# A vision layer on one core: the value weighing and the side work of an attention loop regrouped into four-step packets, and the loop over images written out

## The chip, the core and the metric

The kernel runs on one core of a Trainium2 chip. The metric is the device time of one execution in microseconds (us), lower being better. TensorE is called PE here, VectorE DVE, ScalarE ACT, GpSimd POOL, and SyncE, which issues most DMAs, SP.

## What is computed

Eight images of 3x512x512 are cut into 1024 patches each, embedded to 256 channels, sent through attention with 8 heads, and then through a layer whose second matrix is chosen per token among eight experts:

```python
h = embedded + pos                                   # 8 x 1024 x 256
x = _layernorm(h)                                    # attention's own norm follows
normed = (x - mu) / jnp.sqrt(var + EPS) * ln_gamma + ln_beta
q, k, v = jnp.split(normed @ W_qkv.T, 3, axis=-1)
gate = sigmoid(x @ W_gate.T + b_gate)
scores = jnp.einsum('bhid,bhjd->bhij', q, k) * D ** (-0.5)
attn = softmax(scores, axis=-1)
out = jnp.einsum('bhij,bhid->bhjd', attn, v) * gate  # note: weighs by the row's index i
h = h + x + out @ W_final.T + b_final
H = gelu(layernorm(h) @ W1 + b1)                     # 1024 wide
probs = softmax(H @ Wg + bg);  e = argmax(probs)
h = h + probs[e] * (H @ Wd[e] + bd[e])
```

## The kernel before

Everything is float32; scores, hidden products and the expert products go through PE in its one-pass form (`F32R`), the others as two half products, so that the profile counts two matmuls for each such call. Each engine has its own instruction stream, written by hand in the order in which it runs, and the streams meet by semaphores alone. PE, DVE and ACT take their instructions strictly in that order, so an instruction that waits holds everything behind it.

**The attention loop.** An image `b` has 64 steps `k`: two groups of four heads, eight blocks `i` of 128 rows in each group, four heads `hh`. A step is one chain over three engines. `score(b, k)` on PE makes a 128x1024 block of scores in two banks of PSUM (L477). DVE takes its row maximum (`reduce_max`, L1029). ACT makes the exponentials with their sums (L842). There are two pairs of banks (`SR = 2`), so `score(k)` waits for the exponentials of step `k - 2`. The exponentials stay in SBUF in `pr`, eight blocks deep.

**The weighing.** After four steps (one row block `i`, four heads) DVE divides the values by the sums, `scale_v` (a reciprocal, L945, and a multiply, L948, which raises `vs_ready`). It stands behind the maximum of step `4i + 4` (`SCALE_AT`). PE's `weigh(b, i, j)` for the quarters `j` = 0 to 3 adds `vs.T @ pr` to the output (L491). Each call is four products of 32 columns that run side by side in the array; the text calls one call a block. Quarter 0 waits for `vs_ready`.

**Side work.** The other products that an image needs are laid between the steps by tables. In the first half (k = 0 to 31) stand the projections of the second head group (`QK1_AT`, `project`, L465, in two halves `c`, at k = 0 to 7), and the embedding of the next image (`EMBED_AT`, `embed`, L444, 24 parts at k = 8 to 31). In the second half (k = 32 to 63) stand the gates (`GATE_AT`, L511), the transposes of the next image (`TURN_AT`, `turn`, L456) and its projections for the first head group (`QK0_AT`, L465). They share two spare PSUM banks: part `j` of a kind waits until part `j - 2` has been read. ACT reads a transposed part (`turned`, L772 and L775) and a projection (`high`, L785), in its stream behind the exponentials of the step of the part. DVE makes the rest of a projection (`low`, L936), two steps later (`LOW1_AT`, `LOW0_AT`), and reads a finished embedding (`embedded`, L917).

**Around the steps.** Between k = 31 and 32 stands the router part of the image before (L540 to L576). Between k = 63 and the next image's k = 0 stand `values`, the last weighing (i = 15), the final projection and the first gates. After the last image come the sorting of tokens and 72 slots of expert products, which this change leaves alone.

**The loop over images.** `over_images` writes images 0 and 7 out, and runs a hardware loop of three rounds over two images each between them (1 and 2, 3 and 4, 5 and 6):

```python
body(0, 0, False, True)
with eng.Fori(0, (IMAGES - 2) // 2) as j:
    body(j * 2 + 1, 1, True, True)
    body(j * 2 + 2, 0, True, True)
body(IMAGES - 1, (IMAGES - 1) % 2, True, False)
```

Of the kernel before, what the change touches and what calls it, by code (L numbers as in the profile page):

```python
# [27 lines left out]
IMAGES = 8  # L28
TOKENS = 1024
TILES = TOKENS // P  # L30
# [7 lines left out]
STEPS = HEADS * TILES  # L38
# [9 lines left out]
G_STEPS = STEPS // GROUPS  # L48
# [7 lines left out]
def vit_layer_kernel(nc, x, w_patch, pos_in, pos_w1, pos_w2, pos_bias, ln_gamma, ln_beta, w_qk, w_v,  # L56
# [7 lines left out]
    with ExitStack() as ctx:  # L64
# [149 lines left out]
        def over_images(eng, body):  # L214


            body(0, 0, False, True)
            with eng.Fori(0, (IMAGES - 2) // 2) as j:
                body(j * 2 + 1, 1, True, True)
                body(j * 2 + 2, 0, True, True)  # L220
            body(IMAGES - 1, (IMAGES - 1) % 2, True, False)

        def over_pairs(eng, count, body):

            body(0)
            with eng.Fori(1, count) as j:
# [6 lines left out]
        QK1_AT = {m: divmod(m, 2) for m in range(8)}  # L233
        EMBED_AT = {8 + m: divmod(m, 3) for m in range(24)}
        GATE_AT = {G_STEPS + 3 + m: divmod(m, 2) for m in range(4)}
        TURN_AT = {G_STEPS + 7 + j: j for j in range(8)}
        QK0_AT = {G_STEPS + 17 + 3 * j + c: (j, c) for j in range(4) for c in range(2)}

        LOW1_AT = {k + 2: j for k, (j, c) in QK1_AT.items() if c == 1}
        LOW0_AT = {k + 2: j for k, (j, c) in QK0_AT.items() if c == 1}  # L240
        NORM_AT = {2 + t: t for t in range(TILES)}
        SCALE_AT = {4 * i + 4: i for i in range(15) if i != 7}
        WEIGH_AT = {k: [(i, j) for i in range(15) if i != 7 for j in range(4)
                        if k == min(4 * i + 5 + j // 2 * 2, (i // TILES + 1) * G_STEPS - 1)] for k in range(STEPS)}
# [171 lines left out]
        def _(pe):  # L416
# [202 lines left out]
            def image(b, par, before, after):  # L619
# [15 lines left out]
                for k in range(STEPS):  # L635
# [14 lines left out]
                    score(b, k)  # L650
                    if before and k == G_STEPS + 1:
                        partial_logits(b - 1, 1, 0)
                    if before and k == G_STEPS + 2:
                        turn_logits(b - 1, 1, 1)
                    if k in QK1_AT:
                        j, c = QK1_AT[k]
# [3 lines left out]
                    if after and k in EMBED_AT:  # L660
                        t, part = EMBED_AT[k]
# [3 lines left out]
                    if k in GATE_AT:  # L665
                        hf, c = GATE_AT[k]
# [3 lines left out]
                    if after and k in TURN_AT:  # L670
                        if TURN_AT[k] < 2:
                            wait(pe, "g_tanh", b * 4 + 3 + TURN_AT[k])
                        turn(b + 1, TURN_AT[k])
                    if after and k in QK0_AT:
                        j, c = QK0_AT[k]
# [3 lines left out]
                    for gi, j in WEIGH_AT[k]:  # L679
                        weigh(b, gi, j)  # L680
# [542 lines left out]
```

How the kernel before makes its waits and increments, by code:

```python
        def wait(eng, name, value):  # L201
            if not isinstance(value, int) or value > 0:
                eng.wait_ge(S[name] if isinstance(name, str) else name, value)
# [1 line left out]
        def hold(eng, name, value):  # L206
            if not isinstance(value, int):
                value = eng.to_reg(value)
                eng.wait_ge(S["setup"], 1)
            wait(eng, name, value)
# [36 lines left out]
        @block.sync  # L249
# [50 lines left out]
                    load_rest(b + 1)  # L300
                load_stack(b, 1, before)
                if before:
                    for u in range(4, 16):
                        store_hidden(b - 1, u)
            over_images(sp, image)
            for u in range(16):
                store_hidden(IMAGES - 1, u)
            sp.wait_ge(S["lg_done"], 2 * IMAGES)
            sp.wait_ge(S["h_out"], 16 * IMAGES)
            for i in range(STAGED):
                sp.wait_ge(row_out[i], 16 * IMAGES * 16 // STAGED)
            sp.dma_start(bd_raw[:], b_down).then_inc(S["bd_raw_in"], 16)
            def load_down(j):
                for i in range(WD_BUFFERS):
                    hold(sp, "wd_low", j * WD_BUFFERS + i + 1 - WD_BUFFERS)
                    sp.dma_start(wd_raw[:, i], w_down[j * WD_BUFFERS + i]).then_inc(wd_in[i], 16)
            over_pairs(sp, WD_PIECES // WD_BUFFERS, load_down)
            sp.wait_ge(S["bd_low"], 1)
            sp.wait_ge(S["bd_zero"], 1)
            for part in range(2):
                for e in range(EXPERTS):
```

## Time and profile before

| | |
|---|---|
| median of 3 runs | 1952.97 us (1948.21 to 1954.45) |
| the profiled execution | 1954.93 us, span of the core 1952.8 us |
| PE busy | 1728.6 us, 89% of the span |
| DVE busy | 1151.3 us, 59% |
| ACT busy | 1012.5 us, 52% |
| mean granted TensorE clock | 0.954 of full speed |

The profile gives busy time by engine and line, the stretches between chosen points of the span with the granted clock, and the instructions in order of time. Averages over the span mix stages with different limits; the steps of the attention loop have to be read one stage at a time, by the starts of their scores.

### The profile page before, as it was taken

How to read it: one execution, taken by the hardware profiler on the slowest of the kernel's cores; microseconds unless marked ns; L12 is line 12 of the kernel's file. 1: busy time of each engine (PE TensorE's matmuls, PEld its weight loads, DVE VectorE, ACT ScalarE, POOL GpSimd, SP SyncE). 2: the span in 40 equal slices, each digit the busy share in tenths (PEclk: the TensorE clock that was granted, in tenths of full speed). 3: DMA queues.
4: the chain of work that ended last, by engine and by line, in shares of the span. 5: the costliest groups of instructions: out<-in, count | busy, mean ns of one | idle time of the engine just before them, and what ended most of it. 6: DMA issues, size and time to landing. Idle time of an engine off the chain costs nothing.

```text
span 1952.8 us, 32763 instructions
## 1 busy us (share of the span) xinstructions
PE 1728.6 (89%) x11396; PEld 1180.4 (60%) x11396; DVE 1151.3 (59%) x1899; ACT 1012.5 (52%) x1692; POOL 309.7 (16%) x239
## 2 busy tenths in 40 slices
PE   8587899999998999999899999999797724899998
PEld 4354456646655574566467555745363614899998
DVE  0347767467655856675667468566726278344443
ACT  1144756675574657566746656585666350222222
POOL 0200100200010020002000200200000061455554
PEclk9898999999999999999999999999899867899999
DMA  3133042313413140424033222413040160566663
GB/s 112 34 98 98 1 103 77 125 30 99 112 65 82 63 133 28 103 69 133 18 103 92 93 65 73 129 39 87 17 135 1 60 220 1 200 205 199 208 204 132
DMA packets 68112, 187.59 MB, mean 96 GB/s; under 512 B 14173, under 2 KB 14829, under 8 KB 67824
## 3 DMA queue, kind: packets, MB, share of 16 engines
q1 hardware_dynamic: 51952, 121.48, 22.0%
q0 software_dynamic: 16000, 63.98, 10.0%
q8 instruction: 101, 1.65, 0.4%
q14 instruction: 59, 0.48, 0.1%
HBM read 84.72 MB, written 51.38 MB: 70 GB/s over the span
## 4 chain that ended last, share of the span: by engine, by line
PE 72%; DVE 14%; issue 8%; ACT 4%; DMA 1%; SPq 1%; POOL 0%; DVEq 0%; ACTq 0%; POOLq 0%
PE ps L477 12%; PE ps L738 11%; PE ps L491 10%; PE ps L444 8%; DVE nmax L1029 6%; PE ps L548 3%; PE ps L465 3%; PE ps L726 3%; PE ps L549 3%; PE ps L550 3%; PE ps L527 3%; PE ps L505 3%; PE ps L576 3%; ACT pr L842 2%; DVE oh L1084 2%
## 5 line engine op out<-in xcount | busy, mean ns | idle before, releaser
L1029 DVE TENSOR_REDUCE nmax<-ps 128x1 f32<-128x1024 f32 x512 | 625.2, 1222 | 315.1 <-PE ps L477 305.5
L842 ACT ACTIVATE pr<-ps,nmax 128x1024 f32<-128x1024 f32 x512 | 569.9, 1113 | 295.8 <-DVE nmax L1029 290.6
L477 PE MATMUL ps<-stk,stq 96*128 96x512 f32 x1024 | 407.3, 480 | 80.2 <-ACT pr L842 54.1
L477 PEld LDWEIGHTS ps<-stk,stq 96*128 96x128 f32 x1024 | 168.5, 193 | 282.7 <-ACT pr L842 169.0
L491 PE MATMUL ps<-pr,vs 128*32 128x256 f32 x4096 | 275.9, 391 | 16.7 <-DVE vs L948 16.6
L738 PE MATMUL ps<-wd,hg 128*128 x1728 | 225.5, 287 | 0.0
L339 POOL TENSOR_SCALAR vare<-mv 128x8 f32<-128x8 f32 x24 | 5.7, 238 | 1349.8 <-DVE mv L903 1349.8
L738 PEld LDWEIGHTS ps<-wd,hg 128*128 128x128 f32 x1728 | 212.7, 192 | 0.0
L491 PEld LDWEIGHTS ps<-pr,vs 128*32 128x32 f32 x4096 | 109.8, 110 | 166.6 <-issue 75.5
L879 ACT ACTIVATE hg<-ps 128x512 fp32r<-128x512 f32 x144 | 78.5, 596 | 249.6 <-PE ps L726 249.6
L444 PE MATMUL ps<-wp,xt 128*128 128x256 f32 x768 | 198.3, 385 | 1.6 <-DMA xt<-x_in 0.8
L444 PEld LDWEIGHTS ps<-wp,xt 128*128 128x128 f32 x768 | 146.2, 192 | 32.6 <-DMA xt<-x_in 3.1
L811 ACT ACTIVATE ht<-ps,bf 128x512 f32<-128x512 f32 x128 | 88.3, 690 | 115.5 <-PE ps L550 115.5
L465 PE MATMUL ps<-nt,wqk 128*128 128x512 f32 x256 | 132.3, 602 | 3.9 <-DVE qk L936 3.2
L1148 DVE TENSOR_TENSOR hg<-ps,hg 128x512 fp32r<-128x512 f32 x144 | 93.0, 686 | 48.9 <-ACT hg L879 48.8
L548 PE MATMUL ps<-nt_high,wf 128*128 128x512 f32 x256 | 110.7, 432 | 1.7 <-DVE nt_low L985 1.4
L549 PE MATMUL ps<-nt_low,wf 128*128 128x512 f32 x256 | 101.9, 398 | 0.0
L550 PE MATMUL ps<-nt_high,wf 128*128 128x512 f32 x256 | 101.3, 396 | 0.0
L1155 DVE SCALAR_TENSOR_TENSOR rows<-ps,slot_prob,rows 128x256 f32<-128x256 f32 x72 | 34.8, 484 | 111.1 <-PE ps L740 111.1
L842 ACT ACTIVATION_READ_ACCUMULATOR pr<-ps,nmax 128x1 f32 x512 | 99.5, 194 | 0.0
L404 POOL DMA_INDIRECT out<-rows,slot_to x72 | 72.3, 1004 | 123.2 <-DVE rows L1155 116.3
L726 PE MATMUL ps<-ident,rows 128*128 128x128 f32 x576 | 76.4, 277 | 6.6 <-DMA rows<-token_rows,slot_from 6.6
(123 smaller groups left out, 1944.2 us busy)
## 6 DMA issues: line engine op xcount, KB each, us to landing
token_rows<-staged SPq DMA_DIRECT2D x128, 256.0 KB, 2.0
xt<-x_in SPq DMA_DIRECT2D x64, 384.0 KB, 3.1
stq<-qk SPq DMA_DIRECT2D x192, 128.0 KB, 2.4
stk<-qk SPq DMA_DIRECT2D x192, 128.0 KB, 2.5
token_rows<-hres POOLq DMA_DIRECT2D x8, 1024.0 KB, 5.2
wd_raw<-w_down SPq DMA_DIRECT2D x16, 512.0 KB, 4.0
rows<-token_rows,slot_from POOLq DMA_INDIRECT x72, 4.7
out<-rows,slot_to POOLq DMA_INDIRECT x72, 2.6
```

The source lines that it names most:

```text
L444: last = mm(spare(t)[:, 0:D], xt[:, t % 2, k, :], wp[:, k, :], start=(k == 0), stop=(k == KC - 1))
L465: last = mm(spare(j), wqk[:, c, w * D + g * P:w * D + (g + 1) * P], nt[:, c, hf * HALF:(hf + 1) * HALF], start=(c == 0), stop=(c == DC - 1))
L477: last = mm(ps[:, 2 * (k % SR) + j, :], stq[:, hh, i * P:(i + 1) * P], stk[:, hh, j * 512:(j + 1) * 512], start=True, stop=True)
L491: last = mm(ps[32 * hh:32 * hh + 32, O_BANK + j // 2, (j % 2) * D:(j % 2 + 1) * D], vs[:, gi % 2, hh, :], pr[:, (4 * gi + hh) % PR, j * D: ...
L548: mm(spare(bank), w_high, nt_high[:, c, half], start=(c == 0), stop=False)
L549: mm(spare(bank), w_high, nt_low[:, c, half], start=False, stop=False)
L550: last = mm(spare(bank), w_low, nt_high[:, c, half], start=False, stop=(c == DC - 1))
L726: last = nc.tensor.transpose(ps[:, 2 * (s % 2) + c, q * P:(q + 1) * P], rows[:, s % RING, (4 * c + q) * P:(4 * c + q + 1) * P], ident[:])
L738: mm(o, hg[:, s % 2, h_part, k, :], wd[:, w_part, bass.ds(e, 1), k, :], start=(k == 0 and h_part == w_part), stop=False)
L842: actv(pr[:, k % PR, :], ps[:, 2 * (k % SR):2 * (k % SR) + 2, :].rearrange("p a n -> p (a n)"), ACT.Exp, bias=nmax[:, k % 16:k % 16 + 1], ...
L1029: V.reduce_max(nmax[:, k % 16:k % 16 + 1], ps[:, 2 * (k % SR):2 * (k % SR) + 2, :].rearrange("p a n -> p (a n)"), AX_X, negate=True).then_ ...
L1148: V.tensor_tensor(hg[:, s % 2, 1, 4 * c:4 * c + 4, :].rearrange("p k n -> p (k n)"), ps[:, 2 * (s % 2) + c, :], high_part.bitcast(F32), AL ...
```

## The change

Three things change. Nothing is computed differently, and no instruction that does arithmetic is added or removed.

1. `WEIGH_AT`: the four blocks of a row block's weighing all stand in step `4i + 5`, and right behind its score, ahead of any side work. Before, two stood at the end of step `4i + 5` and two at the end of `4i + 7` (at the end of a half, step 31 or 63 at the latest).
2. Side work moves to the two steps after the pair of scores `4i + 6` and `4i + 7`: it stands in steps 3 and 0 modulo 4. Embedding goes three parts and one part to such a pair of steps, transposes two and one, and a projection or a gate has both its halves in one step.
3. `over_images` is a plain Python loop, so that all eight images are written out and every wait has a constant.

```diff
@@ -213,12 +213,8 @@
 
         def over_images(eng, body):
 
-
-            body(0, 0, False, True)
-            with eng.Fori(0, (IMAGES - 2) // 2) as j:
-                body(j * 2 + 1, 1, True, True)
-                body(j * 2 + 2, 0, True, True)
-            body(IMAGES - 1, (IMAGES - 1) % 2, True, False)
+            for b in range(IMAGES):
+                body(b, b % 2, b > 0, b < IMAGES - 1)
 
         def over_pairs(eng, count, body):
 
@@ -230,18 +226,19 @@
 
 
 
-        QK1_AT = {m: divmod(m, 2) for m in range(8)}
-        EMBED_AT = {8 + m: divmod(m, 3) for m in range(24)}
-        GATE_AT = {G_STEPS + 3 + m: divmod(m, 2) for m in range(4)}
-        TURN_AT = {G_STEPS + 7 + j: j for j in range(8)}
-        QK0_AT = {G_STEPS + 17 + 3 * j + c: (j, c) for j in range(4) for c in range(2)}
-
-        LOW1_AT = {k + 2: j for k, (j, c) in QK1_AT.items() if c == 1}
-        LOW0_AT = {k + 2: j for k, (j, c) in QK0_AT.items() if c == 1}
+        QK1_AT = {k: [(j, 0), (j, 1)] for j, k in enumerate((0, 1, 3, 4))}
+        parts = [divmod(m, 3) for m in range(24)]
+        EMBED_AT = {7 + 4 * q: parts[4 * q:4 * q + 3] for q in range(6)}
+        EMBED_AT.update({8 + 4 * q: parts[4 * q + 3:4 * q + 4] for q in range(6)})
+        GATE_AT = {G_STEPS + 3 + hf: [(hf, 0), (hf, 1)] for hf in range(2)}
+        TURN_AT = {G_STEPS + 7: [0, 1], G_STEPS + 8: [2], G_STEPS + 11: [3, 4], G_STEPS + 12: [5], G_STEPS + 15: [6, 7]}
+        QK0_AT = {G_STEPS + k: [(j, 0), (j, 1)] for j, k in enumerate((16, 19, 23, 27))}
+
+        LOW1_AT = {k + 2: j for k, parts in QK1_AT.items() for j, c in parts if c == 1}
+        LOW0_AT = {k + 2: j for k, parts in QK0_AT.items() for j, c in parts if c == 1}
         NORM_AT = {2 + t: t for t in range(TILES)}
         SCALE_AT = {4 * i + 4: i for i in range(15) if i != 7}
-        WEIGH_AT = {k: [(i, j) for i in range(15) if i != 7 for j in range(4)
-                        if k == min(4 * i + 5 + j // 2 * 2, (i // TILES + 1) * G_STEPS - 1)] for k in range(STEPS)}
+        WEIGH_AT = {4 * i + 5: i for i in range(15) if i != 7}
         assert max(EMBED_AT) < G_STEPS and max(LOW0_AT) < STEPS
 
         block = ctx.enter_context(nc.Block())
@@ -648,36 +645,33 @@
                     if before and k in (G_STEPS, G_STEPS + 1):
                         wait(pe, "hu_read", b * 16 + 2 * (k - G_STEPS) - 2)
                     score(b, k)
+                    if k in WEIGH_AT:
+                        for j in range(4):
+                            weigh(b, WEIGH_AT[k], j)
                     if before and k == G_STEPS + 1:
                         partial_logits(b - 1, 1, 0)
                     if before and k == G_STEPS + 2:
                         turn_logits(b - 1, 1, 1)
-                    if k in QK1_AT:
-                        j, c = QK1_AT[k]
+                    for j, c in QK1_AT.get(k, ()):
                         if j < 2 and c == 0:
                             wait(pe, "g_tanh", b * 4 + 1 + j)
                         project(b, 1, j, c)
-                    if after and k in EMBED_AT:
-                        t, part = EMBED_AT[k]
+                    for t, part in EMBED_AT.get(k, ()) if after else ():
                         if t < 2 and part == 0:
                             wait(pe, "qk_lo", b * 8 + 7 + t)
                         embed(b + 1, t, part)
-                    if k in GATE_AT:
-                        hf, c = GATE_AT[k]
+                    for hf, c in GATE_AT.get(k, ()):
                         if before and hf == 0 and c == 0:
                             wait(pe, "lg_done", b * 2)
                         gates(b, 1, hf, c)
-                    if after and k in TURN_AT:
-                        if TURN_AT[k] < 2:
-                            wait(pe, "g_tanh", b * 4 + 3 + TURN_AT[k])
-                        turn(b + 1, TURN_AT[k])
-                    if after and k in QK0_AT:
-                        j, c = QK0_AT[k]
+                    for j in TURN_AT.get(k, ()) if after else ():
+                        if j < 2:
+                            wait(pe, "g_tanh", b * 4 + 3 + j)
+                        turn(b + 1, j)
+                    for j, c in QK0_AT.get(k, ()) if after else ():
                         if j == 0 and c == 0:
                             wait(pe, "tr_read", b * 8 + 16)
                         project(b + 1, 0, j, c)
-                    for gi, j in WEIGH_AT[k]:
-                        weigh(b, gi, j)
 
             over_images(pe, image)
             for j in range(4):
...
```

In the streams of ACT and DVE the same tables decide where `turned`, `gated_tanh`, `high`, `low` and `embedded` stand; there the loops over a step's parts replace the single part in the same way.

On PE, in the first half of an image, a period of four steps of the embedding stage stood as follows before (L477 score, L444 embedding, L491 weighing, of which x8 are two blocks):

```order
L491 MATMUL ps<-pr,vs 32x256 x8
L477 MATMUL ps<-stk,stq 128x512 x2
L444 MATMUL ps<-wp,xt 128x256 x2
L477 MATMUL ps<-stk,stq 128x512 x2
L444 MATMUL ps<-wp,xt 128x256 x2
```

The five rows are two steps, and four steps are these rows twice. In the changed program four steps read (L474, L441 and L488 are the same lines there):

```order
L474 MATMUL ps<-stk,stq 128x512 x2
L488 MATMUL ps<-pr,vs 32x256 x16
L474 MATMUL ps<-stk,stq 128x512 x4
L441 MATMUL ps<-wp,xt 128x256 x6
L474 MATMUL ps<-stk,stq 128x512 x2
L441 MATMUL ps<-wp,xt 128x256 x2
```

The four blocks have moved directly behind the first score of the period, two scores stand together, three embedding parts follow them, and the fourth part stands in the last step.

The second place is on PE too, in the second half of an image, at steps 43 to 48, where the transposes end and the projections of the next image begin. Before (L456 transpose, L465 half a projection):

```order
L456 MATMUL ps<-ident,n 128x128 x4
L477 MATMUL ps<-stk,stq 128x512 x2
L456 MATMUL ps<-ident,a 128x128 x4
L491 MATMUL ps<-pr,vs 32x256 x8
L477 MATMUL ps<-stk,stq 128x512 x2
L456 MATMUL ps<-ident,a 128x128 x4
L477 MATMUL ps<-stk,stq 128x512 x2
L491 MATMUL ps<-pr,vs 32x256 x8
L477 MATMUL ps<-stk,stq 128x512 x4
L465 MATMUL ps<-nt,wqk 128x512
```

After:

```order
L453 MATMUL ps<-ident,n 128x128 x4
L474 MATMUL ps<-stk,stq 128x512 x2
L488 MATMUL ps<-pr,vs 32x256 x16
L474 MATMUL ps<-stk,stq 128x512 x4
L453 MATMUL ps<-ident,a 128x128 x8
L474 MATMUL ps<-stk,stq 128x512 x2
L462 MATMUL ps<-nt,wqk 128x512 x2
```

Before, two steps without any transpose lay between the last transpose and the first half projection; now the last two transposes stand in step 47 and the whole first projection in step 48, with one score between.

## Rows read from the trace of the kernel before

**Rows 1.** The page's chain of work that ended last, by engine.

```profile
PE 72%; DVE 14%; issue 8%; ACT 4%; DMA 1%; SPq 1%; POOL 0%; DVEq 0%; ACTq 0%; POOLq 0%
```

**Rows 2.** Stretches: start:end, length, busy time by engine, PEclk, DMA share, GB/s.

```profile
273.91:289.49 15.58, 14.29 (x67) 6.48 (x65) 14.25 (x29) 11.04 (x19) 3.01 (x3) 1.00 0.20 68
289.49:333.35 43.86, 43.86 (x318) 29.58 (x314) 32.86 (x46) 27.69 (x47) 0.00 (x0) 1.00 0.18 55
373.25:402.91 29.66, 26.96 (x193) 13.98 (x192) 21.17 (x24) 25.02 (x43) 0.00 (x0) 1.00 0.11 39
402.91:430.57 27.66, 23.94 (x158) 10.58 (x158) 21.30 (x28) 20.13 (x35) 0.00 (x0) 1.00 0.01 1
430.57:451.25 20.68, 20.68 (x123) 15.20 (x123) 8.47 (x17) 5.48 (x9) 0.00 (x0) 1.00 0.79 191
607.85:634.03 26.18, 23.49 (x122) 17.17 (x123) 8.47 (x17) 5.49 (x9) 0.00 (x0) 0.87 0.64 153
969.27:995.94 26.67, 24.62 (x122) 17.34 (x123) 8.46 (x17) 5.49 (x9) 0.00 (x0) 0.81 0.62 150
1366.00:1384.00 18.00, 15.17 (x97) 6.27 (x96) 13.15 (x18) 10.73 (x20) 0.00 (x0) 0.67 0.00 0
1449.35:1502.71 53.36, 41.43 (x305) 17.50 (x303) 40.34 (x47) 39.38 (x65) 0.00 (x0) 1.00 0.06 22
```

**Rows 3.** In order of time, embedding stage of image 1: start, length, engine, line.

```profile
312.73 0.73 PE L477 MATMUL ps<-stk,stq 96*128 96x512 f32 x2
...
313.30 1.03 PE L444 MATMUL ps<-wp,xt 128*128 128x256 f32 x4
313.49 1.23 DVE L1029 TENSOR_REDUCE nmax<-ps 128x1 f32<-128x1024 f32 x1 [0.97 <-PE ps L477]
...
313.97 0.82 PE L477 MATMUL ps<-stk,stq 96*128 96x512 f32 x2
...
314.63 1.03 PE L444 MATMUL ps<-wp,xt 128*128 128x256 f32 x4
314.63 0.17 DVE L945 RECIPROCAL rinv<-rsum 128x4 f32<-128x4 f32 x1
...
314.84 0.29 DVE L948 TENSOR_TENSOR vs<-v,rinv 128x128 f32<-128x128 f32 x1
315.05 1.22 DVE L1029 TENSOR_REDUCE nmax<-ps 128x1 f32<-128x1024 f32 x1
...
315.59 1.07 PE L491 MATMUL ps<-pr,vs 128*32 128x256 f32 x16
...
316.59 0.73 PE L477 MATMUL ps<-stk,stq 96*128 96x512 f32 x2
...
318.50 0.42 DVE L917 TENSOR_TENSOR hres<-ps,posb 128x256 f32<-128x256 f32 x1
```

**Rows 4.** In order of time, image 7, steps with no side work.

```profile
1467.60 0.73 PE L477 MATMUL ps<-stk,stq 96*128 96x512 f32 x2
...
1468.37 1.23 DVE L1029 TENSOR_REDUCE nmax<-ps 128x1 f32<-128x1024 f32 x1 [0.57 <-PE ps L477]
...
1469.09 0.73 PE L477 MATMUL ps<-stk,stq 96*128 96x512 f32 x2 [0.76 <-ACT pr L842]
1469.63 1.11 ACT L842 ACTIVATE pr<-ps,nmax 128x1024 f32<-128x1024 f32 x1 [0.59 <-DVE nmax L1029]
...
1469.75 1.07 PE L491 MATMUL ps<-pr,vs 128*32 128x256 f32 x16
...
1470.64 0.19 ACT L842 ACTIVATION_READ_ACCUMULATOR pr<-ps,nmax 128x1 f32 x1
1470.88 0.30 PEld L477 LDWEIGHTS ps<-stk,stq 96*128 96x128 f32 x2 [0.54 <-ACT pr L842]
```

**Rows 5.** In order of time, a transpose's reader, half a projection, a weighing of four blocks.

```profile
402.76 0.59 ACT L775 ACTIVATE at<-ps 128x512 f32<-128x512 f32 x1
...
405.07 1.02 PE L465 MATMUL ps<-nt,wqk 128*128 128x512 f32 x2
...
435.89 1.93 PE L491 MATMUL ps<-pr,vs 128*32 128x256 f32 x32
```

More of the change, by code:

```diff
@@ L844, in image @@
                          ).then_inc(S["exp_done"], 1)
-                    if after and k in TURN_AT:
-                        turned(b + 1, TURN_AT[k])
-                    if k in GATE_AT and GATE_AT[k][1] == 1:
-                        gated_tanh(b, 1, GATE_AT[k][0])
-                    if k in QK1_AT and QK1_AT[k][1] == 1:
-                        high(b, 1, QK1_AT[k][0])
-                    if after and k in QK0_AT and QK0_AT[k][1] == 1:
-                        high(b + 1, 0, QK0_AT[k][0])
+                    for j in TURN_AT.get(k, ()) if after else ():
+                        turned(b + 1, j)
+                    for hf, c in GATE_AT.get(k, ()):
+                        if c == 1:
+                            gated_tanh(b, 1, hf)
+                    for j, c in QK1_AT.get(k, ()):
+                        if c == 1:
+                            high(b, 1, j)
+                    for j, c in QK0_AT.get(k, ()) if after else ():
+                        if c == 1:
+                            high(b + 1, 0, j)
                 if before:
@@ L1041, in image @@
                         low(b, 1, LOW1_AT[k])
-                    if after and k in EMBED_AT and EMBED_AT[k][1] == 2:
-                        embedded(b + 1, 1 - par, EMBED_AT[k][0])
+                    for t, part in EMBED_AT.get(k, ()) if after else ():
+                        if part == 2:
+                            embedded(b + 1, 1 - par, t)
                     if after and k in LOW0_AT:
```

## The prediction

> **What bounds the kernel now.** I read the page's chain first: PE carries 72% of it and DVE 14% [rows 1], so the order on PE is what counts, but not everywhere. Then I cut one middle image (image 1) at the starts of its scores [rows 2]. Steps 0 to 8 take 15.58 us with PE busy 14.29. Steps 8 to 31, the embedding stage, take 43.86 us with PE busy 43.86: PE alone is the limit. Two steps take 3.86 (score 312.73 to score 316.59 [rows 3]), so four take 7.72, and 11 such pairs with one short step make up the 43.86. Steps 32 to 63 take 29.66 + 27.66 = 57.32 us with PE idle for 6.4. There the limit is the loop through both score banks. Image 7, which has no next image to prepare, shows that loop alone: 53.36 us for 31 steps, 6.89 for four [rows 2]. One turn of it is in [rows 4]: score start 1467.60, maximum at +0.77, exponential at 1469.63, its sums read by 1470.83, the next score in the same banks at 1470.88, so 3.28 us.
>
> **Prices.** From starts to starts on PE [rows 3]: a score costs 0.57 after a weighing (312.73 to 313.30) and 0.66 after an embedding part (313.97 to 314.63), the part 0.67 ahead of a score and 0.96 ahead of a weighing, two blocks 1.00. Four blocks cost 1.86, since the second pair adds 1.93 - 1.07 = 0.86 [rows 5, 3]. A score ahead of a weighing costs 0.66 (1469.09 to 1469.75 [rows 4]), 0.09 more. A part among parts costs 0.87, the 0.96 without that 0.09. On DVE a maximum holds the engine 1.14 (313.49 to 314.63), the scaling 0.42 (to 315.05) with its result 0.50 after its start (314.84 + 0.29). On ACT an exponential takes 1.20 with its sums. Hand-overs cost 0.04 to 0.05.
>
> **Embedding stage after.** Count from the start of score 4i+4. It ends at 0.82, its maximum runs from 0.86, the scaling from 2.00 to 2.50, and the maximum of 4i+5 can start at 2.42. PE: score 0.66, one part 0.67, so score 4i+5 starts at 1.33 and PE is ready to weigh at 1.33 + 0.66 + 0.09 = 2.08. The values come at 2.50, so the weighing starts at 2.55: PE waits 0.47 that it did not wait before, when a part of 0.96 stood in between (weighing then came at 315.59, the values at 315.13 [rows 3]). The weighing ends at 4.41, score 4i+6 takes to 4.98. Score 4i+7 needs the exponential of 4i+5: maximum 2.42 to 3.65, exponential 3.68 to 4.88; just in time. Score to 5.55, three parts 2 x 0.87 + 0.67 = 2.41, next period at 7.96. PE's own work in it is 7.49, less than the 7.72 of before, because there is one way into and out of the 32-column form and not two; the wait eats more than that. In two of the six periods `embedded` stands behind the scaling and pushes the maximum of 4i+5 by 0.42 - 0.08 [rows 3], so score 4i+7 waits 0.28. Sum over 5.7 periods: 5.7 x 0.24 + 0.56 = +1.9 us.
>
> The Trainium skill says, under TensorEngine Tiling (Array Packing), Key Properties, that changing the tiling mode drains TensorE. By that rule alone the merged weighing pays; the trace agrees on the direction with about 0.2 us a period (7.49 against 7.72). It is the rival below that ends faster.
>
> **Steps with no side work after.** Score 4i+6 at 0, 4i+7 at 0.57. Both maxima queue on DVE: 0.77, and 1.91 to 3.14. Exponentials to 3.23 and, behind it, 3.17 to 4.37. Score 4i+8 at 3.28, 4i+9 at 4.42. Maximum of 4i+8 from 4.05, scaling 5.19 to 5.69, weighing from 5.74 (PE was ready at 5.08), next 4i+6 at 7.60. So 7.60 against 6.89: the pair of scores is followed by one wait for a whole turn, and the four blocks stand in the loop in one piece. For 31 steps +5.5 us.
>
> **Second half of a middle image.** The same loop, now with more in it. Gates and the first steps: I take +0.4. In the transpose stage (36 to 48) the third transpose of a packet needs the first to be read, and ACT reads it behind the exponential of the step in between (`turned` stands behind exp(39), exp(43)); that exponential ends 3.6 after its own score (0.77, a queued maximum of 1.6 in all, 1.20), the read takes about 0.6 [rows 5], so PE stands about 1.2 us ahead of `turn` 2 and 5, and the next score, which could have come 0.8 earlier, is late by that. Three periods: +2.3. At step 48 `project` 0 needs transpose 7 read, which ACT does behind exp(47) and `turned` 6. Score 47 at 0; exp(47) ends at 3.6 and the two reads at 4.6; score 48, which needs exp(46), stands at 2.5 and leaves PE ready at 3.1. PE waits 1.5, then both halves of the projection (2 x 0.86, a half being two of the four matmuls that make 1.73; [rows 5] has one half) stand ahead of score 49, which comes 3.65 after score 48. The rest of the period is a score and four blocks 2.6, a wait to score 51 of 0.8, and 2.5: 9.5 in all. Two further periods take 7.60 and the last three steps 7.60 - 2.7 = 4.9 (2.7 being the gap behind a pair, 3.28 - 0.57). 9.5 + 15.2 + 4.9 = 29.6 against 27.66 [rows 2]: +2.0. Sum of the half +4.7.
>
> **Steps 0 to 8.** `project` 2 at step 3 waits for `low` 0 behind the maximum of step 2 and a norm piece on DVE; before, five half projections lay in between. By the same walk score 1 comes at 2.1, 2 at 4.3, 3 at 5.4, `low` 0 is done at 7.3 where PE is ready at 6.0, score 4 at 8.9, 5 at 11.1, 6 at 13.7, 8 at 17.5; before 15.58. I take +2.2, as the walk of the old order comes out 0.6 low.
>
> **Joints.** Before the router, exp(31) comes 0.5 later after its score, because scores 30 and 31 are now together and their maxima queue: +0.5. After step 63 no blocks stand ahead of `values`, and the last weighing, which PE reached 5.3 after the score (430.57 to 435.89 [rows 2, 5]), starts when the values of i = 15 are there, at 4.4: -0.9. The key and query copies that SP issues there still end before PE needs them (PE busy 20.68 of 20.68 [rows 2]).
>
> A middle image: 2.2 + 1.9 + 0.5 + 4.7 - 0.9 = +8.4; six of them +50.4. Image 0, without the router: +8. Image 7: +2.2, 5.7 periods at 0.71 = +4.1, +0.5, +5.5, and +0.6 at its end where the last weighing waits: +12.9. Sum +71.3.
>
> **The loop over images.** Where the hardware loop jumps back, the joint takes 26.18 and 26.67 us against 20.68 between images 1 and 2, which are in one round [rows 2]. Written out, both should be 20.7: -11.5 us. The joints 0 to 1 and 6 to 7, where no jump back happens, are the cover for pricing straight code at nothing. The Trainium skill, Runtime: NRT & Kernel Launch, Instruction fetch mechanics, says that a taken branch to code that is not at hand stalls the fetch; by that rule, the trace agrees with 5.5 and 6.0 us.
>
> **Sum.** 1954.9 + 71.3 - 11.5 = 2014.7 for the profiled execution, which is 2.0 over the median of the runs shown; so 2012.7, I say 2012, +3.0%.
>
> **Rivals.**
> A, the TensorE clock falls more often. PE waits more now, and in image 7 the granted clock was 0.67 for 18 us (between 2.4 and 1.2 GHz) after steps in which PE had begun to wait [rows 2]. A mean of 0.67 is two thirds of the time at the lower level, which doubled part of PE's 15.17 us there: at most 15.17 / 3 = 5 us lost, less where PE waited anyway, so I take 3.5 a fall; once in each of seven images +24: 2036. Against it: steps 32 to 63 of image 7, with PE busy 41.43 of 53.36, kept 1.00. The Trainium skill, TensorE: Matmul & The Clock Gate, says that a PE that idles drops to half its clock; that is this rival. Chance 0.12.
> B, the other side: the values are ready when PE wants them. Then every embedding period falls to PE's own 7.49, and the packets hide the reads of ACT. It is decided in one place, the 2.08 at which PE is ready against the 2.50 of the scaling; if DVE were 0.45 earlier there, 40 periods gain 0.23 (-9), the joints -6, the loop -11.5, and the rest stands at nothing: 1926. Against it: the scaling sits behind a maximum that cannot start before its score ends, and all four prices are in [rows 3]. Chance 0.05.
> C, the straight code fetches badly and the jump's 11.5 us come back or more: 2024 and up. Joints within a round show nothing of it. Chance 0.08.
> D, the walk overrates the waits, each worked out alone, and half of the 71.3 or more is not there: 1977 at half, level with before at a sixth. Against it: the same walk gives the old order 6.75 for steps with no side work, where 6.89 were measured, and PE's 7.7 in the embedding. Chance 0.08, of it 0.03 within 0.3% of before.
> The forecast itself: 0.67.
>
> **Numbers.** Likeliest 2012. The range takes half of the added waits as the low bound (1954.9 + 36 - 11.5, about 1980) and rival A with some of C as the high one (2042). A measurement of this kernel tells about 0.3% (6 us) from no change. Slower 0.92, same 0.03, faster 0.05.
>
> **What would show it.** In the changed trace: embedding periods of 7.9 to 8.3 us, with PE idle ahead of L488 and DVE's values (L945 there) as releaser; pairs of scores 0.57 apart followed by a gap near 2.7 where nothing else stands; PE idle ahead of the third transpose and about 1.5 us ahead of the projection at step 48, released by ACT; all joints near 19.8, and none at 26; the sorting and expert part unchanged. If the periods are at 7.5, the step on the scaling is wrong; if the clock column falls below 1.00 in middle images, it is rival A.

## The result, and the profile after

The changed kernel takes 2058.09 us (median; 2056.44 to 2061.18) against 1953.31 us in the same measurement: a ratio of 1.0544, 95% interval 1.052 to 1.0567. It is slower, as forecast, but by 105 us and not by 59, and above the forecast's upper bound of 2042. Ratios here and below are of undisturbed runs: one run of the kernel before (2253 us) and one of `e3` (3395 us) lie far off and are not in them.

The page of the changed kernel, its busy times, its granted clock over 40 slices of the span, and its chain of work that ended last by engine:

```profile
PE 1752.3 (85%) x11396; PEld 1207.0 (59%) x11396; DVE 1148.2 (56%) x1899; ACT 1009.3 (49%) x1692; POOL 309.7 (15%) x239
...
PEclk9898899999999999999999899999797785999999
...
PE 67%; DVE 16%; issue 11%; ACT 3%; DMA 2%; SPq 1%; POOL 0%; POOLq 0%; DVEq 0%; ACTq 0%
```

No engine has more instructions. DVE and ACT are busy for the same time as before, and PE for 24 us more with the same 11396 matmuls, which is the first sign that some of them ran slower.

The same cuts at the starts of scores as in [rows 2]: image 1 at steps 0, 8, 31, then 32, 48, 63 and the next image's 0; then the joint behind image 2, the second half of image 5, both halves of image 7, and the second half of image 0. The columns are start:end, length, busy time by engine, granted clock, DMA share, GB/s.

```profile
289.93:307.74 17.81, 16.29 (x79) 8.98 (x77) 14.81 (x29) 11.07 (x19) 3.01 (x3) 1.00 0.22 78
307.74:353.12 45.38, 42.85 (x325) 29.32 (x323) 32.28 (x47) 27.33 (x46) 0.00 (x0) 1.00 0.17 53
393.06:426.52 33.46, 27.42 (x195) 14.61 (x193) 21.25 (x24) 24.78 (x42) 0.00 (x0) 0.95 0.10 34
426.52:457.92 31.40, 26.48 (x174) 11.88 (x175) 20.57 (x26) 20.69 (x36) 0.00 (x0) 0.95 0.00 1
457.92:477.67 19.75, 19.46 (x108) 14.77 (x106) 8.98 (x17) 5.30 (x9) 0.00 (x0) 1.00 0.83 196
645.65:665.40 19.75, 19.46 (x108) 14.76 (x106) 8.97 (x17) 5.30 (x9) 0.00 (x0) 1.00 0.82 199
1144.23:1216.54 72.31, 59.85 (x369) 29.50 (x367) 41.90 (x50) 45.68 (x77) 0.00 (x0) 0.86 0.05 16
1424.02:1496.26 72.24, 54.66 (x305) 24.67 (x304) 44.40 (x66) 38.39 (x65) 2.84 (x3) 0.76 0.04 15
1536.49:1606.76 70.27, 53.95 (x320) 24.63 (x319) 39.35 (x46) 39.06 (x65) 0.00 (x0) 0.76 0.05 17
197.99:270.19 72.20, 57.74 (x343) 28.72 (x343) 43.91 (x57) 43.22 (x74) 9.03 (x2) 0.81 0.00 1
```

The first half of the middle image is where the forecast has it: 17.81 for 15.58 and 45.38 for 43.86 [rows 2]. All joints are short now. The second halves are off: 33.46 + 31.40 = 64.86 for 57.32, where the forecast has 62.0, at a clock of 0.95 where it was 1.00. Image 7 is the worst, with 72.24 and 70.27 us at 0.76; its second half took 53.36 at 1.00 before [rows 2].

In order of time, one embedding period of image 1 in the changed kernel (L474 score, L441 embedding, L488 weighing, L1026 maximum):

```profile
323.86 0.82 PE L474 MATMUL ps<-stk,stq 96*128 96x512 f32 x2
...
325.19 0.81 PE L474 MATMUL ps<-stk,stq 96*128 96x512 f32 x2
325.86 0.17 DVE L942 RECIPROCAL rinv<-rsum 128x4 f32<-128x4 f32 x1
...
326.06 0.29 DVE L945 TENSOR_TENSOR vs<-v,rinv 128x128 f32<-128x128 f32 x1
326.27 0.42 DVE L914 TENSOR_TENSOR hres<-ps,posb 128x256 f32<-128x256 f32 x1
326.40 1.93 PE L488 MATMUL ps<-pr,vs 128*32 128x256 f32 x32 [0.41 <-DVE vs L945]
326.60 1.21 DVE L1026 TENSOR_REDUCE nmax<-ps 128x1 f32<-128x1024 f32 x1
...
328.27 1.57 PE L474 MATMUL ps<-stk,stq 96*128 96x512 f32 x4
```

This is the walk of the forecast to within 0.02 us: the second score 1.33 after the first, the weighing at 2.54 (forecast 2.55), released by the values, and the next score at 4.41. The idle time of PE in brackets, 0.41, is a little less than the 0.47 by starts.

The same steps of image 7, which has no side work there:

```profile
1461.88 1.22 DVE L1026 TENSOR_REDUCE nmax<-ps 128x1 f32<-128x1024 f32 x1 [1.37 <-PE ps L474]
...
1463.57 3.64 PE L488 MATMUL ps<-pr,vs 128*32 128x256 f32 x32 [0.54 <-DVE vs L945]
...
1467.14 1.38 PE L474 MATMUL ps<-stk,stq 96*128 96x512 f32 x4
```

The same 32 matmuls take 3.64 us instead of 1.93, and the scores behind them come 3.57 after their start instead of 1.87. That is the lower of TensorE's two levels (1.2 GHz for 2.4). From score 4i+5 to score 4i+6 it is 5.3 here where the forecast has 3.2; all twelve such steps of image 7 at steps 9 to 29 and 41 to 61 take 4.1 to 5.4. In the second halves of images 1 to 3 there are two long ones, 4.15 from score 45 to 46 and 4.86 from 61 to 62, and the other steps of this kind take 2.5 to 3.2; images 4 and 6 have two in other places, and image 5, with 72.31 us, three.

### The profile page after: what moved, and what is told of

Read it like the earlier page. It is cut to its first block, busy times and chain, and to the rows that moved or that the text cites. A ratio compares the mean times of both kernels' runs of the same rounds, so it can differ in the third digit from the quotient of the medians.

```text
span 2055.1 us, 30267 instructions
## 1 busy us (share of the span) xinstructions
PE 1752.3 (85%) x11396; PEld 1207.0 (59%) x11396; DVE 1148.2 (56%) x1899; ACT 1009.3 (49%) x1692; POOL 309.7 (15%) x239
## 4 chain that ended last, share of the span: by engine, by line
PE 67%; DVE 16%; issue 11%; ACT 3%; DMA 2%; SPq 1%; POOL 0%; POOLq 0%; DVEq 0%; ACTq 0%
PE ps L488 12%; PE ps L732 10%; PE ps L474 9%; DVE nmax L1026 7%; PE ps L441 5%; PE ps L462 4%; PE ps L545 3%; PE ps L720 3%; PE ps L546 3%; PE ps L547 3%; PE ps L524 3%; PE ps L508 3%; PE ps L573 2%; DVE oh L1082 2%; PE ps L555 2%
## 5 line engine op out<-in xcount | busy, mean ns | idle before, releaser
L1026 DVE TENSOR_REDUCE nmax<-ps 128x1 f32<-128x1024 f32 x512 | 616.5, 1220 | 433.2 <-PE ps L474 432.0
L474 PE MATMUL ps<-stk,stq 96*128 96x512 f32 x1024 | 404.0, 487 | 101.2 <-ACT pr L836 72.5
L474 PEld LDWEIGHTS ps<-stk,stq 96*128 96x128 f32 x1024 | 175.6, 199 | 285.9 <-ACT pr L836 165.7
L488 PE MATMUL ps<-pr,vs 128*32 128x256 f32 x4096 | 289.4, 431 | 36.0 <-DVE vs L945 35.3
L488 PEld LDWEIGHTS ps<-pr,vs 128*32 128x32 f32 x4096 | 132.3, 121 | 179.5 <-DVE vs L945 74.5
L441 PE MATMUL ps<-wp,xt 128*128 128x256 f32 x768 | 183.9, 384 | 1.9 <-DMA xt<-x_in 1.2
L441 PEld LDWEIGHTS ps<-wp,xt 128*128 128x128 f32 x768 | 147.2, 192 | 28.1 <-DMA xt<-x_in 2.8
L462 PE MATMUL ps<-nt,wqk 128*128 128x512 f32 x256 | 127.2, 623 | 19.0 <-ACT at L769 10.3
L462 PEld LDWEIGHTS ps<-nt,wqk 128*128 128x128 f32 x256 | 48.4, 194 | 63.5 <-issue 32.4
```

What stands on the lines that cost most here:

```text
L441: last = mm(spare(t)[:, 0:D], xt[:, t % 2, k, :], wp[:, k, :], start=(k == 0), stop=(k == KC - 1))
L462: last = mm(spare(j), wqk[:, c, w * D + g * P:w * D + (g + 1) * P], nt[:, c, hf * HALF:(hf + 1) * HALF], start=(c == 0), stop=(c == DC - 1))
L474: last = mm(ps[:, 2 * (k % SR) + j, :], stq[:, hh, i * P:(i + 1) * P], stk[:, hh, j * 512:(j + 1) * 512], start=True, stop=True)
L488: last = mm(ps[32 * hh:32 * hh + 32, O_BANK + j // 2, (j % 2) * D:(j % 2 + 1) * D], vs[:, gi % 2, hh, :], pr[:, (4 * gi + hh) % PR, j * D: ...
L1026: V.reduce_max(nmax[:, k % 16:k % 16 + 1], ps[:, 2 * (k % SR):2 * (k % SR) + 2, :].rearrange("p a n -> p (a n)"), AX_X, negate=True).then_ ...
```

## The experiments

Two theories stood after this. **Theory 1:** the waits of the new order cost what the forecast worked out, some 70 us, and on top of them the clock falls because PE now waits, so that a weighing in one piece runs at half speed inside the loop through the banks. **Theory 2:** something else is slow (the written-out code, or the waits are longer than worked out), and the low clock only goes with it.

### One part of the change at a time

`e1_unroll_only` is the kernel before with this edit alone:

```diff
-            body(0, 0, False, True)
-            with eng.Fori(0, (IMAGES - 2) // 2) as j:
-                body(j * 2 + 1, 1, True, True)
-                body(j * 2 + 2, 0, True, True)
-            body(IMAGES - 1, (IMAGES - 1) % 2, True, False)
+            for b in range(IMAGES):
+                body(b, b % 2, b > 0, b < IMAGES - 1)
```

> The kernel before with the loop over images written out and nothing else. Theory 1 (the added time comes from the new order on PE, the written-out loop gives time back): the two joints of 26.2 and 26.7 us fall to 20.7, so about 1941 us (1938 to 1943). Rival (straight code fetches badly and is part of the 105 us): 1953 or more, with longer joints or holes marked issue between scores.

Measured: 1934.51 us, ratio 0.9903 (0.9879 to 0.9928). Written-out code costs nothing that shows and gives 18 us back, more than the 11.5 forecast. From its windows, the joint behind image 2 and image 7's halves:

```profile
609.14:629.82 20.68, 20.68 (x122) 15.19 (x123) 8.47 (x17) 5.49 (x9) 0.00 (x0) 1.00 0.79 191
1336.39:1390.85 54.46, 42.08 (x288) 17.91 (x286) 45.09 (x67) 38.80 (x65) 2.84 (x3) 1.00 0.06 20
1430.51:1485.03 54.52, 42.74 (x304) 18.11 (x303) 40.24 (x47) 39.33 (x65) 0.00 (x0) 0.97 0.06 21
```

The joint lost its 5.5 us. Image 7's first half, which had taken 57.85 with the clock fall of [rows 2], takes 54.46 at 1.00 here with the same order, while its second half has a fall that it did not have. So in the old order too a fall comes and goes with small shifts, at 1 to 3 us each.

`e2_loop_kept` is the changed kernel with the opposite edit, the hardware loop put back.

> The changed kernel with the hardware loop over images put back. Theory 1: 2058 plus 11 to 14, about 2070 us. Rival: clearly under 2058, if the straight code cost time. If the falls of the TensorE clock (0.95 in the second half of every middle image) depend on where the program happens to stand, they may fall elsewhere here.

Measured: 2070.47 us, ratio 1.06 (1.0579 to 1.0621), 12.4 over the changed kernel. Its two joints behind a jump back take 22.77 and 25.26 us for 19.75. With `e1` this settles the loop: writing it out is a gain under either order, and the tables cost all of the 105 us and the loop's gain besides, 124 us over `e1`.

`e3_weigh_only` has the loop written out and the weighing as changed, but the side work one part to a step:

```diff
-        QK1_AT = {k: [(j, 0), (j, 1)] for j, k in enumerate((0, 1, 3, 4))}
...
+        QK1_AT = {m: [divmod(m, 2)] for m in range(8)}
+        EMBED_AT = {8 + m: [divmod(m, 3)] for m in range(24)}
+        GATE_AT = {G_STEPS + 3 + m: [divmod(m, 2)] for m in range(4)}
+        TURN_AT = {G_STEPS + 7 + j: [j] for j in range(8)}
+        QK0_AT = {G_STEPS + 17 + 3 * j + c: [(j, c)] for j in range(4) for c in range(2)}
```

> Loop written out, the four blocks of a weighing right behind the score of step 4i+5, but all side work one part to a step as before. Theory 1 says that the late values and the four blocks in one piece are most of the cost: by the same walk over a period as in the prediction, some +75 us at full clock over the kernel before, less 12 for the loop, so 2015 us, plus what falls of the clock cost. Rival (the packets of side work are what costs): near 1960.

Measured: 2041.86 us, ratio 1.0455 (1.0428 to 1.0483). The weighing in one piece behind the score is by itself a loss of 107 us over `e1`, and the rival's 1960 is ruled out.

`e4_side_only` has the packets, and the weighing two and two blocks at the end of a step:

```diff
-        WEIGH_AT = {4 * i + 5: i for i in range(15) if i != 7}
+        WEIGH_AT = {k: [(i, j) for i in range(15) if i != 7 for j in range(4)
+                        if k == min(4 * i + 5 + j // 2 * 2, (i // TILES + 1) * G_STEPS - 1)] for k in range(STEPS)}
...
-                    if k in WEIGH_AT:
-                        for j in range(4):
-                            weigh(b, WEIGH_AT[k], j)
...
+                    for gi, j in WEIGH_AT[k]:
+                        weigh(b, gi, j)
```

> Loop written out, side work in packets as in the changed kernel, but the weighing two and two blocks at the end of steps 4i+5 and 4i+7 as before. In the embedding stage three parts and two blocks then stand behind one score (2.6 + 1.0 us), and two scores follow nearly together once per period only with nothing to hide their loop. Theory 1 by the walk: +120 us over before, less 12, about 2060. Rival (the merged weighing alone makes the cost and packets are free): near 1945.

Measured: 2066.8 us, ratio 1.0577 (1.0552 to 1.0602). Each part loses by itself about as much as the two together (107 and 132 over `e1` for 124). The embedding stage of image 1 (steps 8 to 31) shows how they belong to each other; first `e3`, then `e4`:

```profile
299.54:348.53 48.99, 45.08 (x330) 30.31 (x331) 33.69 (x48) 28.21 (x47) 0.00 (x0) 1.00 0.16 50
```

```profile
313.58:364.82 51.24, 44.09 (x310) 27.86 (x306) 32.83 (x44) 26.50 (x44) 0.00 (x0) 1.00 0.16 47
```

Against 43.86 before and 45.38 with both. Over `e1`'s 43.85, the one part costs 5.1 us and the other 7.4 in this stage at full clock, and the two together 1.5: each repairs most of what the other costs.

The two parts lose in different ways, which image 7 shows. Its first and second half in `e3`:

```profile
1410.22:1479.02 68.80, 53.31 (x305) 24.10 (x303) 44.12 (x66) 38.54 (x65) 2.84 (x3) 0.78 0.05 16
1520.53:1589.18 68.65, 52.74 (x320) 23.59 (x319) 39.41 (x46) 39.04 (x65) 0.00 (x0) 0.78 0.05 17
```

and in `e4`:

```profile
1469.76:1527.00 57.24, 43.25 (x288) 18.55 (x286) 45.16 (x67) 38.70 (x65) 2.84 (x3) 0.97 0.06 19
1566.67:1623.10 56.43, 44.90 (x305) 19.12 (x303) 40.24 (x47) 39.43 (x65) 0.00 (x0) 0.91 0.06 21
```

With the merged weighing alone, image 7 is nearly as long and as low in its clock as in the changed kernel. With the packets alone it is not, and what `e4` loses it loses mostly at a clock of 1.00, in the first halves of images 1 to 6 (70.3 to 72.0 us for 59.3) and in second halves of 62.5 for 56.8.

### Work added where PE waits

`e5_filler` adds work to the changed kernel: products of a zero matrix with constant weights, added to the output banks, at the places where PE waits.

```diff
...
+            def fill(n):
+                for _ in range(n):
+                    mm(ps[:, O_BANK, :], zero[:], wf1[:, 0, 0, 0:512], start=False, stop=False, skip_group_check=True)
...
                     score(b, k)
+                    if after and k in (40, 44, 48):
+                        fill(4)
...
+                    if after and 39 <= k <= 60:
+                        fill({39: 4, 43: 4, 47: 4, 51: 2, 52: 2, 55: 2, 56: 2, 59: 2, 60: 2}.get(k, 0))
+                    if not after and (7 <= k <= 28 or 39 <= k <= 60):
+                        fill({3: 8, 0: 2}.get(k % 4, 0))
```

> The changed kernel with work added: products of a zero matrix with constant weights (128x512, one pass, about 0.23 us each) are added to the output banks, 8 behind a pair of scores that has no side work (image 7) and 2 in the step after, 4 or 2 at the steps of the second half where PE waits. They change no value. Theory 1 with its new part (over half of what the forecast missed is TensorE's clock, which falls to its lower level after steps in which PE waits): the clock stays at 1.00, steps with a weighing at 4.1 to 5.3 us go back to 2.5 to 3.2, second halves of middle images from 64.9 to about 61.5, both halves of image 7 from 72 and 70 to about 60: 2058 falls to about 2000 us. Rival (the long steps come from waits, and the lower clock is only their companion): no gain, or slower than 2058, since PE has more to do.

Measured: 2007.43 us, ratio 1.0282 (1.0265 to 1.0299). With more work in it the kernel is 51 us faster than the changed one. Its windows, image 1's second half and image 7's halves:

```profile
389.29:450.93 61.64, 58.32 (x405) 31.94 (x403) 41.78 (x50) 45.56 (x77) 0.00 (x0) 1.00 0.05 19
1396.51:1457.09 60.58, 54.43 (x365) 30.51 (x363) 44.17 (x66) 38.40 (x65) 2.84 (x3) 1.00 0.05 18
1498.61:1557.38 58.77, 53.51 (x381) 30.08 (x379) 39.08 (x46) 39.06 (x65) 0.00 (x0) 1.00 0.05 20
```

and its period of image 7 in order of time (L619 are the added products, L489 the weighing):

```profile
1430.50 0.73 PE L475 MATMUL ps<-stk,stq 96*128 96x512 f32 x2
...
1431.84 1.93 PE L489 MATMUL ps<-pr,vs 128*32 128x256 f32 x32 [0.60 <-DVE vs L957]
...
1433.70 1.24 PE L475 MATMUL ps<-stk,stq 96*128 96x512 f32 x4
...
1434.78 2.04 PE L619 MATMUL ps<-wf,zero 128*128 128x512 f32 x8
```

The clock is 1.00, the weighing is back at 1.93, and the wait on the values (0.60 for 0.54) is as it was: the order's own waits stay, and what the clock took is gone. Theory 2 would have had this run at 2058 or above. Of the gain, image 7 gives 23 us, image 5's second half 10.6, image 0's second half 7.0, and the other five second halves 3.1 to 3.2 each. Some 7 us go back in stretches where the clock falls here and did less or not at all in the changed kernel (the first halves of images 0 and 1, and the stretches from score 31 to 32 of images 5 to 7).

`e9_filler_last_image` keeps the last two of these added lines alone, so that only image 7 is filled.

> The changed kernel with the zero products in image 7 alone. By the clock theory image 7's halves go from 72.2 and 70.3 to the 60.6 and 58.8 of the run with all fillers, some 23 us in all, and the other images keep their clock of 0.95 in the second half: 2035. If the fall is not a local matter of the steps in which PE waits, other images move too.

Measured: 2033.98 us, ratio 1.0417 (1.0386 to 1.0448), 24 under the changed kernel, with image 7 at 60.60 and 58.78 us. The effect is in the image that is filled. Its windows, image 1's second half and image 7's first:

```profile
390.03:457.79 67.76, 55.62 (x368) 27.20 (x367) 41.82 (x50) 45.57 (x77) 0.00 (x0) 0.92 0.05 17
...
1420.52:1481.12 60.60, 54.45 (x365) 30.50 (x363) 44.18 (x66) 38.41 (x65) 2.84 (x3) 1.00 0.05 18
```

The second halves of images 1 to 6 stay low, at 64.8 to 67.8 us. They are not quite those of the changed kernel: image 1's was 64.86 there, and image 5's falls from 72.31 to 64.75 with nothing added to it. So single falls move, here with a program that is the same up to image 7 but for the zeroing of the added matrix.

### The same waits in the old order

`e11_idle_in_old_order` is `e1` with one longer wait per four steps, in image 7 alone:

```diff
+                if b == IMAGES - 1 and k % 4 == 2:
+                    wait(pe, "exp_done", b * STEPS + k)
-                if k >= SR:
+                elif k >= SR:
                     wait(pe, "exp_done", b * STEPS + k - SR + 1)
```

> The old order with the loop written out, and in image 7 one added wait per four steps: score 4i+2 waits for the exponential of the step just before it, so that PE stands idle in longer pieces, as it does in the packets, while its work and its order stay. At full clock the walk gives 7.75 for four steps against 6.75, so image 7's halves become about 60 us each and the whole about 1948. The clock theory says that the clock falls in image 7 as in the changed kernel (0.76), with halves of 65 to 72: 1960 or more. If it is the four blocks in one piece, and not PE's waiting, that brings the fall, the clock stays at 0.97 to 1.00 and the time at 1948.

Measured: 1956.89 us, ratio 1.0032 (1.0016 to 1.0048), 22 over `e1`, a little under the 1960 that the clock theory named. Its windows of image 7, both halves, and then two stretches of the first half (one at a low clock, one where the clock was up):

```profile
1333.91:1400.26 66.35, 49.72 (x289) 21.86 (x288) 44.11 (x66) 38.43 (x65) 2.84 (x3) 0.82 0.05 16
1440.51:1505.95 65.44, 48.20 (x304) 21.33 (x303) 39.25 (x46) 39.01 (x65) 0.00 (x0) 0.84 0.05 18
```

```profile
1350.00:1369.00 19.00, 15.25 (x97) 6.54 (x96) 12.98 (x18) 10.37 (x18) 0.00 (x0) 0.65 0.00 0
1369.00:1379.00 10.00, 6.21 (x51) 2.69 (x44) 6.04 (x8) 6.28 (x12) 0.00 (x0) 0.99 0.01 2
```

The clock fell, 0.82 and 0.84 for 1.00 and 0.97 in `e1`, with the weighing in two pieces and every instruction in its old place. So PE's waiting is enough to bring the fall, without the weighing in one piece. The fall of the stretch from 1350 to 1369 begins in a pause of PE of 1.62 us, the longest in that stretch, and the weighing of two blocks takes 1.94 us there, where it takes 1.07 at full clock:

```profile
1356.49 2.07 PE L475 MATMUL ps<-stk,stq 96*128 96x512 f32 x4 [1.62 <-ACT pr L840]
1358.49 1.94 PE L489 MATMUL ps<-pr,vs 128*32 128x256 f32 x16
```

 The size of the wait was off: at full clock the period is 8.12 (1370.59 to 1378.71, scores of equal place), not 7.75, because the maximum of step 4i+5 also stands behind the scaling. So 31 steps at full clock are 63, and the clock's own part is some 3 us a half here, where it is 11 to 12 in the changed kernel (72.24 for 60.58). A weighing of two blocks that runs at half speed loses 0.9, one of four 1.7. So the time of this run decides little between the two theories (it is the fastest of its ten executions, 1950.95 us, that is profiled); the clock column does.

### Three that gave nothing

`e8_part_between` moves one embedding part of each packet to between score 4i+5 and its weighing, where PE waits for the values:

```diff
-        EMBED_AT.update({8 + 4 * q: parts[4 * q + 3:4 * q + 4] for q in range(6)})
+        EMBED_AT.update({9 + 4 * q: parts[4 * q + 3:4 * q + 4] for q in range(6)})
...
-                    if k in WEIGH_AT:
+                    if k in WEIGH_AT and k not in EMBED_AT:
...
+                    if k in WEIGH_AT and k in EMBED_AT:
+                        for j in range(4):
+                            weigh(b, WEIGH_AT[k], j)
```

> The changed kernel with one embedding part of each packet moved from behind score 4i+4 to between score 4i+5 and its weighing. It tests the term of 0.47 us a period: PE has 0.87 us of work while the values are made ready. If the term is right, the embedding periods fall from 7.90 to about 7.5, the 45.4 us of steps 8 to 31 to about 43.3, some 15 us in all: 2043. If PE was not really held by the values there, nothing changes.

Measured: 2055.26 us, ratio 1.052 (1.0502 to 1.0537), not told apart from the changed kernel. Its embedding stage:

```profile
306.97:351.89 44.92, 43.42 (x325) 28.98 (x323) 32.11 (x46) 27.35 (x46) 0.00 (x0) 1.00 0.17 54
```

44.92 for 45.38: taking the wait on the values away gives 0.5 of the 2 us expected. The periods are 7.9 as before (0.94, 3.46, 0.57, 2.91 for the four steps from score 4i+4 on). Most of what the values held is now held by the pair: two maxima stand in a row on DVE, so that the exponentials of the second score come late, and the second score behind them waits for ACT, some 0.3 us a period:

```profile
316.39 0.73 PE L474 MATMUL ps<-stk,stq 96*128 96x512 f32 x2 [0.16 <-ACT pr L839]
```

`e6_before_filler` adds one or two zero products per step to `e1`, in image 7 and in the second half of image 0. `e10_fill_dma_wait` adds 14 to `e1` in image 0 ahead of step 32.

```diff
+                    if (not after and (8 <= k <= 28 or 38 <= k <= 60)) or (not before and 38 <= k <= 60):
+                        fill(1 if k % 2 or after else 2)
```

```diff
+                        else:
+                            for _ in range(14):
+                                mm(spare(0), ones[:], wf1[:, 0, 0, 0:512], start=True, stop=True)
```

> The order of before with the loop written out (1934.5 us) and one or two of the same zero products at each step of image 7 and in the second half of image 0, the only halves of the old order whose clock fell. By the clock theory the falls there go away: image 0's second half 59.6 to 57.5, and 3 to 5 us in all where the products fit into the waits: about 1931. If the products do not fit they add up to 0.2 us a step, some 10 us: 1945.

> The old order with the loop written out (1934.5 us) and 14 products into a spare bank in image 0, where PE waits some 7 us for the second half's copies ahead of step 32. By the clock theory the steps behind that wait start at the higher clock: image 0's second half from 59.6 to about 57.3, 1932. If a wait of PE does not bring the fall, no change, 1934.5.

Measured: 1940.5 us (ratio 0.9942, 0.9926 to 0.9959) and 1938.66 us (0.9936, 0.9913 to 0.9958), neither better than `e1`'s 1934.51; both expectations of a gain missed. In `e6` image 7 has its clock at 1.00 in both halves but takes 0.9 us longer in the first, where `e1` had no fall, and 0.3 in the second, where it had one: with waits this short the products cost at least what they save. (The expectation also calls these the only halves of `e1` whose clock fell; image 1's second half had fallen too, 59.49 us at 0.97.)

In image 0 the products stood in the wrong place or were too few. PE's wait ahead of step 32 is 12.42 us in `e1` and not the 7 of the expectation, and the 14 products of `e10` leave 8.94 of it. The clock is at its lower level from step 32 on, for 11.66 us in `e1`, 9.03 in `e10`, and 9.39 in `e6`, where it is back at 1.00 before the first added product, at step 38:

```profile
193.84 2.07 PE L473 MATMUL ps<-stk,stq 96*128 96x512 f32 x4 [12.42 <-DMA stk<-qk]
```

```profile
194.67 2.07 PE L473 MATMUL ps<-stk,stq 96*128 96x512 f32 x4 [8.94 <-DMA stk<-qk]
```

```profile
195.31:204.70 9.39, 6.00 (x11) 2.98 (x12) 7.66 (x12) 3.75 (x7) 7.39 (x2) 0.50 0.00 0
204.70:255.59 50.89, 48.25 (x341) 26.05 (x340) 36.70 (x45) 39.02 (x68) 1.65 (x1) 1.00 0.01 1
```

(`e1`, then `e10`, then `e6`.) `e10` gets 1.1 us from it (58.43 for 59.55) and loses 3.1 in image 5's second half, where a fall has come that `e1` does not have. No version here has a lower median than the plain written-out old order; `e10` is not clearly told apart from it.

## Why the prediction was off, step by step

Each term of a middle image's sum, against image 1 of the changed kernel and of `e5_filler`, where the clock stays up in all but the first row (both less [rows 2]):

| step | forecast | changed kernel | with the waits filled |
|---|---|---|---|
| steps 0 to 8 | +2.2 | +2.2 | not comparable: a fall lies in it |
| embedding, 8 to 31 | +1.9 | +1.5 | +1.5 |
| 32 to 63 | +4.7 | +7.5 | +4.3 |
| joint behind 63 | -0.9 | -0.9 | -0.9 |

- **What bounds the kernel** was right: PE in the embedding, the loop through the banks elsewhere. The order's waits were priced well: images 2, 3 and 4 of `e5` take 8.0 us more than those of `e1`, joints counted, for the +8.4 forecast, and image 7's second half takes 58.77 for the 58.9 of the walk. `e5` less `e1` is 72.9 us and the forecast's sum 71.3, but that they agree so closely is partly luck: `e5` still has falls in images 0 and 1, and its image 0 is 9.8 us over that of `e1` for the 8 forecast.
- **The wait on the values** is there at the forecast size (weighing at 2.54 against 2.55), but it is not worth what it lasts: in `e8`, with work laid into it, the pair of scores takes its place and 0.5 of 2 us is gained. Rival B, with DVE itself earlier, was not run.
- **The projection at step 48 and the third transpose** wait as described, 0.98 to 1.16 us for the 1.2 and 1.37 for the 1.5 forecast; at full clock the half adds 4.3 for the 4.7 forecast (steps 32 to 48 +2.1 for 2.7, steps 48 to 63 29.85 us for 29.6). In the changed kernel, at steps 44 and 48 of image 1:

```profile
418.69 0.63 PE L453 MATMUL ps<-ident,n 128*128 128x128 f32 x4 [0.98 <-ACT at L769]
...
428.62 1.99 PE L462 MATMUL ps<-nt,wqk 128*128 128x512 f32 x4 [1.37 <-ACT at L769]
```

- **The joint before the router**, +0.5, is off: 39.94 for 39.90 at image 1, +0.1 at most.
- **The loop over images**, -11.5, was the right mechanism and too small: the two joints fell as forecast, and `e1` gave 18 (19.5 between the profiled executions). Of what the joints don't explain there, falls of the clock that moved gave some 3 net (3.4 in image 7's first half), and some tenths in each image and a little behind the last image the rest. Under the new order it gave 12.4.
- **What failed is the clock**, which the sum put at nothing and rival A at "3.5 a fall; once in each of seven images" with a chance of 0.12. It is the case that came in, and at 51 us (2058 less `e5`), not 24; with the waits filled the kernel takes 2007, near the 2012 forecast. The price for a middle image came out right by luck, from another sum: in image 1's second half two steps with a weighing are hit, 1.65 us each, 3.2 more than in `e5` in all. What was wrong is how often the clock falls in the halves without side work. In image 7 all twelve such steps (9 to 29 and 41 to 61) are hit, by 0.95 to 2.2 us each, and the two halves lose 23 us where the forecast has 3.5; images 0 and 5 lose 7.0 and 10.6 in their second halves.
- **Two premises of rival A** led there. It took the lost time from the old order, where a fall doubles two blocks at a time and partly inside waits; the changed kernel has four blocks in one piece on the path that sets the period, so each weighing that is hit costs some 1.7 us. And it held the 1.00 of image 7's second half against the rival, although that was a stretch in which PE was busy 41.43 of 53.36 us, and the forecast's own walk had just stretched about the same work to 59 us.

What stays open: at what share or length of PE's waiting the clock begins to fall. Single falls move between stretches from one profiled execution to the next (image 5's second half took 72.31 us in the changed kernel, 64.7 in `e8` and 64.75 in `e9`, which leave it as it is), and no run here tells why that one was long.

## What to carry to other kernels

When a change makes PE wait in a stage where it still does much of the work, price the change twice: once at the clock of the profile, and once with the longest piece of PE work in the loop at half speed in every period. For image 7 this gives 12 times 1.7, an estimate of 20 us for the 23 lost. Work on the critical path did better here in small pieces: falls of the clock cost some 3 us a half in `e11` and 11 to 12 in the changed kernel. To learn whether the clock or the order is at fault, fill the waits with products that change nothing: if the kernel gets faster with more work, and its own products get shorter, it was the clock. Look first where the wait is that the fall follows, and how long it is.

## What the runs showed of the hardware

- Adding some 60 zero products to each half of image 7 made that half 12 us faster (72.24 to 60.58, and 70.27 to 58.77), by keeping the granted clock at 1.00 where it was 0.76.
- The clock fell to 0.65 over 19 us in a stretch where PE was busy 15.25 of them (`e11`), with no pause of PE longer than 1.62 us in it. In image 7 of the changed kernel, at 0.76, none is longer than 2.1 us.
- The jump back of the hardware loop cost 5.5 and 6.0 us a time here, with a granted clock of 0.87 and 0.81 across it [rows 2]; in straight code with the same order (`e1`) the joint is 20.67 or 20.68 every time. In the new order it cost 3.0 and 5.5 (`e2`), at 0.93 and 0.86.
